# A graph-attention kernel: the first dense product as three rounded products, its operands transposed one tile ahead, the residual weights loaded later, TensorE's prologue reordered

## The chip, the cores and the metric

The kernel runs on one core of one Trainium2 chip. The metric is the device time of one execution in microseconds (us), the median of several executions.

## The reference

A graph has 1250 nodes of 768 features and 40,000 edges `(src, dst)`, to which one self loop per node is added. Two blocks follow each other, each `x = layernorm(x + block(x))`.

```python
x_norm = layer_norm(x, norm_g, norm_b)
out1 = gat_conv(x_norm, src, dst, W1, a_src1, a_dst1, b1, 4, 192, N)   # 4 heads
out2 = gat_conv(out1, src, dst, W2, a_src2, a_dst2, b2, 2, 96, N)      # 2 heads
block0 = concatenate([x, out2]) @ Wu + bu
# gat_conv: h = x @ W; e = leaky_relu(s_src[src] + s_dst[dst]);
#           softmax of e over the edges of one dst; sum of alpha * h[src]
h = relu(gcn_conv(x, W1, b1)); block1 = gcn_conv(h, W2, b2)   # second block
```

## The kernel before

The nodes are padded to T = 10 tiles of 128. The edges are turned into a dense matrix of counts, `ct`, of 1280 x 1280, which every later stage reads. All engines run one program each, written out in order, and meet at semaphores; what follows names the stages in order of time.

**Prologue.** SP loads W1 in two halves, small vectors, W2 (`w2x`), x (`xs`) and the upper 768 rows of Wu (`wux`). TensorE (`block.tensor`) transposes W1 into `w1T` (ScalarE copies each piece out of PSUM), transposes the edge keys (`keys()`, after VectorE has made `diag`), and forms twelve pieces of `wp` = W1 times W2 (n = 0 to 11, four PSUM banks in turn), which ScalarE copies to SBUF. VectorE works out which edge units each group needs (`cand` to `rngi`) and the layer norm of tile 0 (`moments`, `scales`; ScalarE's square root is `deviations`).

**Counting loop.** `tile(q)` runs for q = 0 to 9 with GPT = 4 groups w each. In a group VectorE writes one-hot matrices of edges (`one_hots`: `hots_*` and `hotd_*` for two windows of three edge units, then `xohs`, `xohd` for units that did not fit, in a loop whose length is read from `rngrow`). TensorE multiplies them into counts (`edge_group`), ScalarE copies the counts out (`ctmp`). Four windows of one-hots can be ready ahead of TensorE. Between the groups TensorE does the dense product of the tile, normalised x (transposed as `xT`) times `wp`, a quarter after each group: three products of 128x128 by 128x388 in float32, whose result `dense_out` copies to `g`. In the last tile the product is done in two halves after groups 0 and 1. At the head of a tile TensorE transposes the normalised rows `xh` (`normal_transposes`), and ScalarE scales them into `xT` (`transposed`); after group 0 TensorE transposes the counts of the tile before (`count_transposes`), of which ScalarE makes `mask` (`counts_out`). In its last group VectorE waits for the last `dense_out` (`source_scores`, `svec`).

**Between the loop and the heads.** VectorE runs `maxima(h)` for heads 0 to 3: ten instructions each (L590) that read two SBUF tensors, `src_row` and `mask`, back to back; `maxima(h)` needs the broadcast rows of head h, which TensorE makes (`source_rows`) and ScalarE copies. In TensorE's order these rows alternate with the residual product x times Wu (`x_wu(q)`, q = 0 to 4 with `wux`): source_rows of head 0, `x_wu(0)`, source_rows of head 1, and so on. Before `x_wu(0)` TensorE waits for `wu_plus`: GpSimd adds the identity to the six diagonal blocks of `wux` (L505), one instruction each, once it has landed. The first head's third tile on VectorE (`n == EARLY`) waits for `x_wu(4)`, since `att` takes the place of `wux`.

**Heads and second block.** Six attention heads (VectorE, ScalarE and TensorE in turn), then the graph convolution, in which each float32 product is already three products of rounded operands (`split_product`): high x high, high x low, low x high, with float32r operands.

## Time and profile before

| | |
|---|---|
| median of 3 runs | 799.88 us (799.39 to 800.42) |
| the profiled execution's own time | 799.75 us |
| its span | 798.0 us |
| TensorE (PE) busy | 753.3 us, 94% |
| VectorE (DVE) busy | 564.5 us, 71% |
| ScalarE (ACT) busy | 321.8 us, 40% |
| GpSimd (POOL) busy | 27.2 us, 3% |

The busy times are of the whole span; the counting loop takes about a fifth of it, and what limits it has to be read there. A float32 matmul appears as two records, a float32r one as one. "PEclk" is the granted TensorE clock as a share of the full one. In rows of the timeline the bracket names the idle time ahead of the instruction and what ended it; records overlap, so the pace is read from start to start.

### The profile page before, as it was taken

How to read it: one execution, taken by the hardware profiler on the slowest of the kernel's cores; microseconds unless marked ns; L12 is line 12 of the kernel's file. 1: busy time of each engine (PE TensorE's matmuls, PEld its weight loads, DVE VectorE, ACT ScalarE, POOL GpSimd, SP SyncE). 2: the span in 40 equal slices, each digit the busy share in tenths (PEclk: the TensorE clock that was granted, in tenths of full speed). 3: DMA queues.
4: the chain of work that ended last, by engine and by line, in shares of the span. 5: the costliest groups of instructions: out<-in, count | busy, mean ns of one | idle time of the engine just before them, and what ended most of it. 6: DMA issues, size and time to landing. Idle time of an engine off the chain costs nothing. (4 is left out here: it accounts for less than half of the span.)

```text
span 798.0 us, 12011 instructions
## 1 busy us (share of the span) xinstructions
PE 753.3 (94%) x4363; PEld 655.2 (82%) x4363; DVE 564.5 (71%) x972; ACT 321.8 (40%) x638; POOL 27.2 (3%) x41
## 2 busy tenths in 40 slices
PE   4899999998999989999998998899999999999997
PEld 2877677766666989999855888799999999999996
DVE  3498988872999999999689999695644332403554
ACT  2647767673533334444154454562203331301000
POOL 7100000000000020000000020000000000000000
PEclk8999999998989999999999999899999999999999
DMA  9400000000000231010000510100000003000111
GB/s 310 166 2 2 2 2 1 2 2 1 1 0 1 70 131 67 2 67 1 0 1 1 187 30 1 41 1 1 1 1 1 1 1 120 0 1 1 65 75 56
DMA packets 10673, 28.17 MB, mean 35 GB/s; under 512 B 675, under 2 KB 4079, under 8 KB 10100
## 3 DMA queue, kind: packets, MB, share of 16 engines
q1 hardware_dynamic: 9924, 27.04, 9.6%
q8 instruction: 38, 0.62, 0.3%
q10 hardware_dynamic: 688, 0.32, 0.2%
q14 instruction: 23, 0.19, 0.1%
HBM read 23.48 MB, written 3.88 MB: 34 GB/s over the span
## 5 line engine op out<-in xcount | busy, mean ns | idle before, releaser
L1260 PE MATMUL ps<-g,att 128*128 128x193 f32 x800 | 133.3, 328 | 3.7 <-DVE att L720 2.3
L1260 PEld LDWEIGHTS ps<-g,att 128*128 128x128 f32 x800 | 130.3, 190 | 6.5 <-DVE att L720 2.9
L1092 ACT ACTIVATE att<-att,ssrc 128x1250 f32<-128x1250 f32 x60 | 80.2, 1338 | 99.0 <-DVE att L759 98.8
L759 DVE SCALAR_TENSOR_TENSOR att<-uB,s 128x1250 f32<-128x1250 f32 x60 | 90.5, 1513 | 0.0
L1260 PE MATMUL ps<-wp,xT 128*128 128x388 f32 x240 | 87.5, 502 | 2.6 <-ACT xT L975 2.6
L1260 PE MATMUL ps<-ctr,yhi 128*128 128x512 f32 x360 | 88.1, 353 | 0.1
L720 DVE SCALAR_TENSOR_TENSOR att<-att,ct 128x1250 f32<-128x1250 f32 x60 | 87.2, 1454 | 0.7 <-ACT att L1092 0.5
L861 DVE TENSOR_TENSOR ylo_a<-ps,yhi 128x512 fp32r<-128x512 f32 (+2 forms) x34 | 16.1, 528 | 77.4 <-ACT yhi L943 77.4
L1260 PE MATMUL ps<-ctr,ylo_a 128*128 128x512 f32 (+3 forms) x288 | 70.2, 352 | 0.1
L1260 PEld LDWEIGHTS ps<-ctr,yhi 128*128 128x128 f32 x360 | 64.1, 188 | 6.0 <-issue 0.4
L1260 PEld LDWEIGHTS ps<-wp,xT 128*128 128x128 f32 x240 | 42.6, 190 | 26.1 <-issue 3.7
L1260 PEld LDWEIGHTS ps<-ctr,ylo_a 128*128 128x128 f32 x288 | 51.0, 188 | 5.2 <-DVE ylo_a L854 0.4
L943 ACT ACTIVATE yhi<-ps 128x384 fp32r<-128x384 f32 (+2 forms) x36 | 16.3, 529 | 95.6 <-PE ps L1260 95.6
L1260 PE MATMUL ps<-h2x,att 128*128 128x97 f32 x400 | 48.1, 277 | 4.2 <-DVE att L720 2.8
L1260 PEld LDWEIGHTS ps<-h2x,att 128*128 128x128 f32 x400 | 46.0, 192 | 6.9 <-DVE att L720 5.9
L1260 PE MATMUL ps<-wux,xTd 128*128 128x384 f32 x120 | 40.8, 500 | 0.7 <-ACT xTd L943 0.7
L1260 PE MATMUL ps<-wux,xT 128*128 128x384 f32 x120 | 40.9, 497 | 0.0
L1260 PE MATMUL ps<-gw2lo,yhi 128*128 128x384 f32 x120 | 40.6, 338 | 0.0
L1260 PE MATMUL ps<-gw2hi,yhi 128*128 128x384 f32 x120 | 40.4, 337 | 0.0
L1260 PE MATMUL ps<-gw1lo,yhi 128*128 128x384 f32 x120 | 40.2, 335 | 0.0
L899 DVE SCALAR_TENSOR_TENSOR hpre<-ps,dinv,gb1b 128x384 f32<-128x384 f32 x20 | 12.4, 618 | 37.8 <-PE ps L1260 37.8
L1260 PEld LDWEIGHTS ps<-wux,xTd 128*128 128x128 f32 x120 | 23.3, 197 | 16.6 <-issue 2.3
(244 smaller groups left out, 1332.3 us busy)
## 6 DMA issues: line engine op xcount, KB each, us to landing
uB<-u_dram SPq DMA_DIRECT2D x4, 1280.0 KB, 5.9
wux<-in_L_gnn_Wu SPq DMA_DIRECT2D x2, 2304.0 KB, 15.2
gw<-in_L_gnn_W SPq DMA_DIRECT2D x2, 2304.0 KB, 10.7
xs<-in_x SPq DMA_DIRECT2D x1, 3456.0 KB
out<-ybuf SPq DMA_DIRECT2D x9, 384.0 KB, 2.3
w<-in_L_gnn_W SPq DMA_DIRECT2D x2, 1152.0 KB, 7.8
w2x<-in_L_gnn_W SPq DMA_DIRECT2D x1, 576.0 KB, 9.8
wuo<-in_L_gnn_Wu SPq DMA_DIRECT2D x1, 576.0 KB
```

The costliest lines, as they stand in the source:

```text
L720: v.scalar_tensor_tensor(a, a, HUGE, ct[:, q, 0:N], ALU.min, ALU.mult).then_inc(att_ready, 1)
L759: v.scalar_tensor_tensor(att[:, att_place(n), 0:N], uB[:, hp % 2, 1, 0:N], s08[:, h, q:q + 1], uB[:, hp % 2, 0, 0:N], ALU.add, ALU.max).th ...
L861: last = v.tensor_tensor(rows, place(f, k)[:, a0 * P - span[0]:a1 * P - span[0]].rearrange("p (t n) -> p t n", n=P), yhi[:, a0:a1, f * P:( ...
L899: v.scalar_tensor_tensor(hpre[:, n % 2, :], ps[:, H_RING[n % 4], 0:HALF], dinv[:, q:q + 1], gb1b[:, k * HALF:(k + 1) * HALF], ALU.mult, AL ...
L943: a.activation(dst, src, ACT.Copy, **kw).then_inc(done, 1)
L1092: a.activation(at_, at_, ACT.Exp, bias=ssrc[:, h, q:q + 1]).then_inc(att_exp, 1)
L1260: return t.matmul(o, lhsT, rhs, start=start, stop=stop, **kw)
```

## The change

The dense product of the counting loop is done as three products of rounded operands. ScalarE's copy of a piece of the weights now rounds to `wphi`, and VectorE subtracts it from PSUM to get `wplo` (`weights_low`, twelve pieces, in the prologue; a bank is free for the next piece only then). For x, ScalarE makes `xThi` by one more copy, and VectorE makes `xTlo` (`x_low`, once per tile, after group 0). The normalised rows are transposed and scaled during the tile before (after group 1 on TensorE, ahead of group 2's outputs on ScalarE). The moments of tiles 1 and 2 move from the loop into the prologue. On TensorE the transposes of the edge keys stand behind both halves of W1, and the two products with `diag` behind the small vectors. `wplo` takes the room of `wux`, so the load of `wux` waits until the last dense product is done. Line numbers of the changed kernel are about 35 higher (the helper L1260 is L1296, L590 is L625 or so).

```diff
+            xin = t_in["x"]
+            sp.dma_start(xs[:, 0, :], xin[0:P, :]).then_inc(x0_in, 16)
             sp.dma_start(w2x[:, :, 0:C1], t_in["L0_gnn_W2"].rearrange("(j p) n -> p j n", p=HC)).then_inc(w2_in, 16)
-            xin = t_in["x"]
-            sp.dma_start(xs[:, 0:T - 1, :], xin[0:(T - 1) * P, :].rearrange("(t p) n -> p t n", p=P)).then_inc(x_in, 16)
+            sp.dma_start(xs[:, 1:T - 1, :], xin[P:(T - 1) * P, :].rearrange("(t p) n -> p t n", p=P)).then_inc(x_in, 16)
             sp.wait_ge(pad_set, 2)
             sp.dma_start(xs[0:NR, T - 1, :], xin[(T - 1) * P:N, :]).then_inc(x_in, 16)
-            sp.dma_start(wux[:, :, :], t_in["L0_gnn_Wu"][0:D, :].rearrange("(k p) n -> p k n", p=P)).then_inc(wux_in, 16)
             sp.wait_ge(rng_ready, 1)
             sp.dma_start(rngrow[0:1, :], rngi[:, :]).then_inc(rng_row_in, 16)
+            sp.wait_ge(dn_ps, 2 * T)
+            sp.dma_start(wux[:, :, :], t_in["L0_gnn_Wu"][0:D, :].rearrange("(k p) n -> p k n", p=P)).then_inc(wux_in, 16)
...
+            def weights_low(n0, n1):
+                for n in range(n0, n1):
+                    k, hh = n // 2, n % 2
+                    v.wait_ge(wp_out, n + 1)
+                    v.tensor_tensor(wplo[:, k, 2 * hh:2 * hh + 2, :], ps[:, n % 4, 0:2 * GW].rearrange("p (h n) -> p h n", h=2),
+                                    wphi[:, k, 2 * hh:2 * hh + 2, :].bitcast(F32), ALU.subtract).then_inc(wplo_out, 1)
+            def x_low(q):
+                x32, low, high = (xT0[:, :, :], xT0lo[:, :, :], xT0hi[:, :, :]) if q == 0 else (xT[:, q % 2, :, :], xTlo[:, q % 2, :, :], xThi[:, q % 2, :, :])
+                v.wait_ge(xhi_out, q + 1)
+                v.tensor_tensor(low, x32, high.bitcast(F32), ALU.subtract).then_inc(xlo_out, 1)
...
+            v.wait_ge(const_b, 1)
+            v.wait_ge(x0_in, 16)
+            moments(0, 1)
             v.wait_ge(keys_t, 1)
             v.tensor_copy(sloT[:, :, :].rearrange("p a c -> p (a c)"), ps[:, 5, 0:EC]).then_inc(keys_out, 1)
+            v.wait_ge(keys_t, 2)
...
+            weights_low(0, 1)
...
+            weights_low(1, 2)
...
+            scales(0, 1)
+            weights_low(2, 6)
             v.wait_ge(x_in, 32)
-            moments(0, 1)
-            scales(0, 1)
+            moments(*pair(0))
+            weights_low(6, 8)
+            scales(*pair(0))
+            v.memset(svec[:, :].bitcast(F32), 0.0)
+            v.memset(uvecs[:, :].bitcast(F32), 0.0)
+            v.tensor_tensor(sel[:, :], identf[0:VR, 0:H1 * T], identf[0:VR, VLO:VR], ALU.add)
+            weights_low(8, 2 * KD)
...
-                    if win == RING - 1:
-                        v.wait_ge(wp_out, 2 * KD)
...
-                    if q < T // 2 and w == 0:
+                    if w == 0:
+                        x_low(q)
+                    if 0 < q < T // 2 and w == 0:
                         moments(*pair(q))
-                    if q < T // 2 and w == 2:
+                    if 0 < q < T // 2 and w == 2:
...
+                a.wait_ge(tp_out, 2 * q + 2)
+                copy(high, dst, xhi_out)
+            deviations(0, 1)
             for k in range(KD):
                 for hh in range(2):
                     n = 2 * k + hh
                     a.wait_ge(wp_ps, n + 1)
-                    copy(wp[:, k, 2 * hh:2 * hh + 2, :], ps[:, n % 4, 0:2 * GW].rearrange("p (h n) -> p h n", h=2), wp_out)
-                    if n == 7:
-                        deviations(0, 1)
-                    if n == 8:
-                        a.wait_ge(x_in, 32)
+                    copy(wphi[:, k, 2 * hh:2 * hh + 2, :], ps[:, n % 4, 0:2 * GW].rearrange("p (h n) -> p h n", h=2), wp_out)
+                    if n == 5:
+                        a.wait_ge(x0_in, 16)
                         a.wait_ge(rstd_ready, 1)
                         a.activation(xh0[:, :], xs[:, 0, :], ACT.Identity, bias=nmr[:, 0:1], scale=rstd[:, 0:1]).then_inc(xh_ready, 1)
-                    if n == 10:
-                        transposed(0, xT0)
-            a.wait_ge(wp_out, 2 * KD)
+                    if n == 8:
+                        a.wait_ge(rng_ready, 1)
+                        transposed(0, xT0[:, :, :], xT0hi[:, :, :])
+                    if n == 9:
+                        deviations(1, 3)
...
+            a.wait_ge(wplo_out, 2 * KD)
...
-                if q > 0:
-                    transposed(q, xT[:, r, :, :])
                 for w in range(GPT):
-                    if q < T // 2 and w == 1:
+                    if 0 < q < T // 2 and w == 1:
                         deviations(2 * q + 1, min(2 * q + 3, T))
-                    if w == GPT - 1 and not last:
+                    if w == 0 and not last:
                         a.wait_ge(rstd_ready, q // 2 + 2)
-                        fixed_place(q + 1, 1 - r)
+                        fixed_place(q + 1)
+                    if w == 2 and not last:
+                        transposed(q + 1, xT[:, 1 - r, :, :], xThi[:, 1 - r, :, :])
...
+            t.wait_ge(const_a, 1)
+            t.wait_ge(keys_made, 1)
+            for gi in range(EG):
+                t.transpose(ps[:, 4, gi * P:(gi + 1) * P], shir[:, gi, :], identf[:, :])
+                last = t.transpose(ps[:, 5, gi * P:(gi + 1) * P], slor[:, gi, :], identf[:, :])
+            last.then_inc(keys_t, 1)
...
+            t.wait_ge(diag_ready, 1)
+            for k in range(2):
+                last = mm(ps[0:NG, 6 + k, 0:EG * P], ones[:, 0:NG], diag[:, k, :], True, True)
+            last.then_inc(keys_t, 1)
...
-                if k == 2:
-                    t.wait_ge(keys_out, 1)
                 for hh in range(2):
                     n = 2 * k + hh
                     if n >= 4:
-                        t.wait_ge(wp_out, n - 3)
+                        t.wait_ge(wplo_out, n - 3)
...
-                    if n == 9:
-                        t.wait_ge(rng_ready, 1)
+                    if n == 7:
+                        t.wait_ge(keys_out, 1)
                         normal_transposes(0, xh0)
...
-                if q > 0:
-                    t.wait_ge(cp_deg, 3 * q + 1)
-                    normal_transposes(q, xh[:, r, :])
+                high, low = (xT0hi[:, :, :], xT0lo[:, :, :]) if q == 0 else (xThi[:, r, :, :], xTlo[:, r, :, :])
                 if q == 1:
                     t.wait_ge(cst_out, 1)
                 for w in range(GPT):
...
                         cs = range(KD) if last else range(3 * (w % 2), 3 * (w % 2) + 3)
                         if 0 in cs:
                             t.wait_ge(dn_out, 2 * q + k + 1)
-                        t.wait_ge(tp_out, 2 * q + (1 if cs[-1] < 3 else 2))
+                        t.wait_ge(xlo_out, q + 1)
                         for c in cs:
-                            step = mm(ps[:, 2 + k, 0:2 * GW], xT0[:, c, :] if q == 0 else xT[:, r, c, :], wp[:, c, 2 * k:2 * k + 2, :], c == 0, c == KD - 1, skip_group_check=True)
+                            mm(ps[:, 2 + k, 0:2 * GW], high[:, c, :], wphi[:, c, 2 * k:2 * k + 2, :], c == 0, False, skip_group_check=True)
+                            mm(ps[:, 2 + k, 0:2 * GW], high[:, c, :], wplo[:, c, 2 * k:2 * k + 2, :], False, False, skip_group_check=True)
+                            step = mm(ps[:, 2 + k, 0:2 * GW], low[:, c, :], wphi[:, c, 2 * k:2 * k + 2, :], False, c == KD - 1, skip_group_check=True)
                         if cs[-1] == KD - 1:
                             step.then_inc(dn_ps, 1)
                     if w == 0 and behind:
                         t.wait_ge(tp_out, 2 * q + 2)
                         count_transposes(q - 1, 1 - r)
+                    if w == 1 and not last:
+                        t.wait_ge(cp_deg, 3 * q + 4)
+                        normal_transposes(q + 1, xh[:, :])
```

TensorE's queue, one group of the first tile and what follows it, before (rows of `order` carry the name of the output and the inputs):

```order
L1260 MATMUL ps<-identb 128x2x16
L1260 MATMUL ps<-wp,xT_65 128x388 x3
L1260 MATMUL ps<-hotd_b,hots_b 128x160 x6
L321 TENSOR_LOAD rngrow
L1260 MATMUL ps<-hotd_c,hots_c 128x160 x6
```

And the same place now:

```order
L1296 MATMUL ps<-identb 128x2x16
L1296 MATMUL ps<-wphi,xT0hi 128x388 [waits xlo_out,dn_out]
L1296 MATMUL ps<-wplo,xT0hi 128x388
L1296 MATMUL ps<-wphi,xT0lo 128x388
L1296 MATMUL ps<-wphi,xT0hi 128x388
```

Three products have become nine, of three operand pairs in turn, and the first waits for VectorE's `x_low`.

SP's queue from the load of W2 on, before:

```order
L426 DMA w2x<-in_L_gnn_W 96x8x192
L428 DMA xs<-in_x 128x9x768
L430 DMA xs<-in_x 98x768 [waits pad_set]
L431 DMA wux<-in_L_gnn_Wu 128x6x768
L433 DMA rngrow<-rngi 1x40x2 [waits rng_ready]
```

And now:

```order
L434 DMA xs<-in_x 128x768
L435 DMA w2x<-in_L_gnn_W 96x8x192
L436 DMA xs<-in_x 128x8x768
L438 DMA xs<-in_x 98x768 [waits pad_set]
L440 DMA rngrow<-rngi 1x40x2 [waits rng_ready]
L442 DMA wux<-in_L_gnn_Wu 128x6x768 [waits dn_ps]
```

The first tile of x comes ahead of W2, and `wux` has moved behind a wait that ends with the last dense product. VectorE's queue in a tile of the loop now, between the last one-hot of group 0 and the first of group 1:

```order
L630 TENSOR_TENSOR xohd<-vkey,key 128x320
L654 ISA
L654 COMPARE_AND_BRANCH
L542 TENSOR_TENSOR xTlo<-xT,xThi 128x768 [waits xhi_out]
L548 BN_STATS stats<-xs 128x6 x4
```

The row of L542 is new; before, the moments (tiles 1 to 4) or the next one-hot followed at once.

## Rows read from the trace of the kernel before

**Rows 1.** Timeline of TensorE in a late tile: start, length, engine, line, instruction.

```profile
120.32 2.19 PE L1260 MATMUL ps<-wp,xT 128*128 128x388 f32 x6 [0.17 <-ACT xT L975]
122.35 1.25 PE L1368 MATMUL ps<-identf,ctmp 128*128 128x128 f32 x10
...
134.65 2.19 PE L1260 MATMUL ps<-wp,xT 128*128 128x388 f32 x6 [0.17 <-ACT xT L975]
```

**Rows 2.** Busy time in stretches: PE, PEld, DVE, ACT, POOL, clock, DMA.

```profile
90.00:105.30 15.30, 14.90 (x100) 10.54 (x100) 13.64 (x35) 10.49 (x29) 0.00 (x0) 1.00 0.01 2
```

**Rows 3.** VectorE's waits, 39.28 to 180: total us, times, longest.

```profile
DVE xohs L594 <- issue: 7.7, 32, 0.6
...
DVE hots_b L594 <- PE ps L1260: 3.2, 5, 1.2
DVE hots_a L594 <- PE ps L1260: 1.8, 5, 0.6
DVE rstd L571 <- ACT sd L968: 1.5, 2, 0.9
DVE xohs L594 <- PE ps L1260: 0.8, 2, 0.6
```

**Rows 4.** Timeline of VectorE at both ends of the loop.

```profile
39.28 0.56 DVE L594 TENSOR_TENSOR hots_a<-iota,sloT 128x768 bf16<-128x768 bf16 x1 [0.55 <-DVE key L632]
...
179.76 0.33 DVE L595 TENSOR_TENSOR xohd<-vkey,key  x1
```

**Rows 5.** Timeline of TensorE in the second block's split product.

```profile
609.72 0.34 PE L1260 MATMUL ps<-gw1hi_b,yhi 128*128 128x384 f32 x1
...
614.96 0.33 PE L1260 MATMUL ps<-gw1hi_a,yhi 128*128 128x384 f32 x1
```

**Rows 6.** Instructions by tile `gw`: ns min/median/max, first and last start.

```profile
L806 DVE TENSOR_TENSOR gw1lo<-gw,gw1hi_a x4: 948/952/953, 566.0 to 568.6; 128x768 fp32r<-128x768 f32 x4
```

**Rows 7.** Timeline of TensorE in the last tile.

```profile
184.78 4.16 PE L1260 MATMUL ps<-wp,xT 128*128 128x388 f32 x12
...
195.21 0.20 PE L1260 MATMUL ps<-identb 128*128 128x32 bf16 x1
```

**Rows 8.** Timeline of the prologue.

```profile
16.33 0.45 PE L1276 MATMUL ps<-identf,shir 128*128 128x128 f32 x1 [5.16 <-DVE diag L532]
...
20.44 2.83 PE L1292 MATMUL ps<-identf,w 128*96 128x128 f32 x24
...
24.94 13.40 PE L1260 MATMUL ps<-w2x,w1T 96*128 96x194 f32 x80 [0.45 <-ACT acol L943]
...
42.41 1.94 DVE L560 BATCH_NORM_STATS2 stats<-xs 128x6 f32<-128x384 f32 x4
```

**Rows 9.** Timeline between the loop and the first head.

```profile
198.22 1.46 DVE L590 CUSTOM_DVE_ANT_0 scrap<-ssB_a,mask 128x1250 bf16<-128x1250 f32 x1 [3.87 <-ACT ssB_a L943]
...
201.81 7.98 PE L1260 MATMUL ps<-wux,xTd 128*128 128x384 f32 x24 [0.67 <-ACT xTd L943]
...
213.65 1.46 DVE L590 CUSTOM_DVE_ANT_0 scrap<-ssB_a,mask 128x1250 bf16<-128x1250 f32 x1
...
245.72 8.87 PE L1260 MATMUL ps<-wux,xTd 128*128 128x384 f32 x27
...
255.12 0.16 DVE L758 MEMSET att<- 128x120 f32 x1
```

**Rows 10.** Timeline of GpSimd's second set of adds and VectorE meanwhile.

```profile
290.18 4.40 POOL L505 TENSOR_TENSOR wux<-wux,identf 128x128 f32<-128x128 f32 x6 [257.88 <-DMA wux<-in_L_gnn_Wu]
...
290.75 1.46 DVE L720 SCALAR_TENSOR_TENSOR att<-att,ct 128x1250 f32<-128x1250 f32 x1
```

**Rows 11.** Instructions by tile `wux`: ns min/median/max, first and last start.

```profile
L505 POOL TENSOR_TENSOR wux<-wux,identf x12: 449/453/2337, 29.8 to 294.1; 128x128 f32<-128x128 f32 x12
```

**Rows 12.** DMA issues, 655 to 680: size, us to landing.

```profile
gw<-in_L_gnn_W SPq DMA_DIRECT2D x1, 2304.0 KB, 8.3
```

**Rows 13.** Busy time behind the loop's end; columns as in Rows 2.

```profile
195.00:200.00 5.00, 4.99 (x25) 4.80 (x24) 1.78 (x3) 1.91 (x4) 0.00 (x0) 0.50 0.00 0
```

More of the change, by code:

```diff
@@ L519, in _, with moments @@
             S, Dn = edges[:, :, 0, :], edges[:, :, 1, :]
+            def weights_low(n0, n1):
[8 more added lines that the diff above has]
+                v.tensor_tensor(low, x32, high.bitcast(F32), ALU.subtract).then_inc(xlo_out, 1)
+            def moments(q0, q1):
+                for q in range(q0, q1):
+                    for k in range(2):
+                        last = v.bn_stats(stats[:, q, k, :], xs[:, q, k * HALF:(k + 1) * HALF])
+                last.then_inc(stats_own, 1)
+                v.wait_ge(stats_own, (q0 + 1) // 2 + 1)
+                for q in range(q0, q1):
+                    last = v.bn_aggr(mv[:, q, :], stats[:, q, :, :])
+                last.then_inc(var_ready, 1)
             v.wait_ge(const_a, 1)
@@ L1297, in _ @@
             t.transpose(ps[0:HC, 1, 0:3 * NJ], arows[:, :], identf[0:3 * NJ, 0:3 * NJ]).then_inc(vec_t, 1)
+            t.wait_ge(diag_ready, 1)
+            for k in range(2):
+                last = mm(ps[0:NG, 6 + k, 0:EG * P], ones[:, 0:NG], diag[:, k, :], True, True)
+            last.then_inc(keys_t, 1)
             t.wait_ge(vec_out, 1)
```

65 lines of the change are left out of this document (24 added, 41 removed).

## The prediction, before the run

> **What bounds the kernel now.** The busy shares say TensorE (94%), but they are a mean over stages, so I read the counting loop by itself first. The timeline of TensorE shows a late tile [rows 1]: the next one begins 134.65 - 120.32 = 14.33 us on, almost without a gap, so there TensorE sets the pace. An early tile takes 15.30 us, of which VectorE is busy 13.64 [rows 2]; the rest of it is mostly VectorE's own gaps, 7.7 / 32 = 0.24 us ahead of each `xohs` with no engine to wait for [rows 3]. So tiles 1 to 4 run at VectorE's pace already, and over the whole loop it waits for others only 3.2 + 1.8 + 1.5 + 0.8 = 7.3 us [rows 3]. From its first one-hot at 39.28 to the end of the last tile's third group at 179.76 + 0.33 = 180.1 it needs 140.8 us [rows 4]. TensorE is some way behind and ends the last dense product at 184.78 + 4.16 = 188.9; the loop ends at 195.4, 6.5 us later [rows 7]. After it VectorE runs `maxima` back to back, and TensorE alternates rows and `x_wu` [rows 9]. At the third tile of the first head both arrive together: `x_wu(4)` ends at 245.72 + 8.87 = 254.6, VectorE is there at 255.12 [rows 9]. TensorE's slack between loop and heads is 0.5 us.
>
> **The dense products.** Three float32 products take about 2.04 us (122.35 - 120.32) [rows 1], 0.68 each. The second block does the same three-product form with 384 columns: 30 records from 609.72 to 614.96, 0.175 each [rows 5]. Nine are 1.57 us, so a quarter is 0.46 us shorter, and 40 quarters (ten tiles of four) 18.6 us. ScalarE's `xT` for the first quarter, 0.17 us late per tile now [rows 1], is ready a tile ahead. This is all TensorE's time, and it counts only as far as VectorE can follow.
>
> **What VectorE gets.** `x_low` is one subtraction of 128x768 from SBUF per tile. The same form on `gw` starts three more times in 568.6 - 566.0 us, 0.87 each [rows 6]; I take 0.9, ten times, +9.0 us. In six tiles (0 and 5 to 9) it fills a gap of 0.24 that stood there: -1.4. The moments of tiles 1 and 2 leave the loop: 1.94 [rows 8] and about 0.5 for the small operations behind them, -2.4. Waits for TensorE and ScalarE vanish, 7.3 us over 14 times, but the twelve on TensorE fall back to the usual gap: -(7.3 - 12 x 0.24) = -4.4. Sum for the stretch of 140.8: 141.6 us. In a tile VectorE then needs 14 to 16 us and TensorE about 12.2 (14.33 less 4 x 0.46 and 0.17), so VectorE sets the pace throughout.
>
> **The prologue.** TensorE was idle 5.16 us before the keys [rows 8]. Now the second half of W1 (2.83 us) fills that, ending at 14.0; keys and `diag` took 20.44 - 16.33 = 4.1 us [rows 8], so the pieces of W1 x W2 begin at 18 to 19 instead of 24.94. Each takes 13.40 / 10 = 1.34 us [rows 8]. The ninth ends, with the six transposes put ahead of it, at about 31; behind its copy ScalarE scales `xT0`, rounds it, copies another piece and takes the square root (about 4.5 us, one after another); VectorE waits for that, then has the small operations and four subtractions of 0.45: about 38.0, and with key and register loads the first one-hot at 38.8, 0.5 earlier. Six us on TensorE become half a us on VectorE. Bounds: 37.8 and 40.5 (if the clock falls in between).
>
> **The loop's end.** The third group of the last tile is ready at 38.8 + 141.6 = 180.4, the second 3.1 us (a quarter of VectorE's tile without extras) before. Around it TensorE has a first half (18 products, 3.15 us), the transposes of counts (1.25 [rows 1]), a group (1.0) and the second half (3.15); from the first group of the tile, 174.5, that makes 183.0 against 188.9. The rest, 6.5 us, stays. So the loop ends 6 us earlier (bounds 3 and 8.5).
>
> **Where it is given back.** `wux` used to be there since the prologue. Now SP issues it when the last dense product is done, 183.1. A load of the same size with the queues free lands 8.3 us after its issue [rows 12]: 191.4. VectorE begins `maxima(0)` 198.22 - 188.94 = 9.3 us after the dense product [rows 9], at 192.3. GpSimd has six adds, 2.5 us where nothing disturbs them (median 453 ns, shortest 449) [rows 11], so only two are done when `maxima(0)` begins. What then? One add took 2337 ns, and it is the first of the second set [rows 11]: it began at 290.18, and 2.34 - 0.45 = 1.9 us later, 292.1, is the time at which the VectorE instruction of 290.75 ended, 292.2 [rows 10]. That instruction read two SBUF tensors, as the one before it did. GpSimd had been waiting since before 290.75 and still did not get in between the two. `maxima(0)` is ten such instructions end to end, 13.9 us. I therefore take the four adds left as held up until 206.2 and done at 207.9.
>
> The Trainium skill ("SBUF — State Buffer", Who interferes with whom) says that a VectorE instruction with two SBUF inputs and a GpSimd one that reads SBUF exclude each other for one instruction at a time. By that alone GpSimd would get its turn after each of the ten, which is the third case below and gives about 798; the row shows a turn that it did not get.
>
> TensorE would have begun `x_wu(0)` at 201.81 - 6 = 195.8; it begins at 207.9, 6.1 us later than before. It was idle for 12 us, and behind a lesser lull the granted clock was 0.50 for 5 us [rows 13], so up to 1.8 us more. The rows of head 1 stand behind `x_wu(0)` in TensorE's queue: they are out 7.5 + 2.3 us after 207.9, at 217.7 to 219.5, against VectorE's old start of `maxima(1)` at 213.65 [rows 9], +4 to +6. TensorE reaches the end of `x_wu(4)` 6.1 to 7.9 us later, less the slack of 0.5. I take +6.2 for the first head; from there all is as before. 799.75 + 6.2 = 806 us. The profiled execution (799.75, span 798.0) is within 0.2 us of the median of 799.88, so the sum serves for both.
>
> **Rivals.**
> (1) GpSimd is not held up, or keeps its turn once it has it, since its adds begin 0.8 us before `maxima(0)`. Then `wux` is complete 8.4 + 2.5 = 10.9 us after the dense product, and TensorE asks for it only at 201.81 - 188.94 = 12.9: the 6 us stay. At worst VectorE waits 1.8 us for the last four adds. 793.8 to 795.6; I write 794.5. For it: nothing shows this very instruction (L590) against GpSimd. This is the case on the other side; it decides at whether the sixth add is done within 12.9 us. Chance 0.30.
> (2) GpSimd gets one add in after each instruction of `maxima(0)`: four times 1.38 + 0.42 = 7.2, complete at 16.6 after the dense product, 3.7 late for TensorE, up to 1.8 for the clock: -6 + 3.7 to 5.5, 797.5 to 799.3. Chance 0.12.
> (3) TensorE still sets the loop, or VectorE's gaps shrink with the waits: at most 18.6 + 2 us less, 779, or the same less 13 if the adds are held up. Against it stands [rows 2]. Chance 0.03.
> (4) The loop gains nothing: with the half clock of [rows 13] in the early tiles, where TensorE would be idle about 3 us behind each `x_low` and the moments, and no hold-up later. 799 to 803. Against it: four windows ready ahead let TensorE make it up. Chance 0.07.
> (5) The forecast, 804 to 808. Chance 0.48.
>
> **How the numbers follow.** The likeliest is (5), 806, with a range of its own of 803 to 809 (loop bounds 3 and 8.5, clock 0 or 1.8). The 80% range must reach rival (1): 793 to 808.5. A measurement of this kernel tells about 0.2% (1.6 us) from no change. Faster: (1), (3), half of (2): 0.40. Same: half of (2), part of (4): 0.09. Slower: (5) and the rest of (4): 0.51.
>
> **What the profile after would show.** Right: nine records of `wphi`/`wplo` per quarter in 1.57 us; VectorE over 93% busy in the loop with gaps only of its own, PE waiting for DVE in each tile; the loop's end near 189.5; `wux` landing 8 to 9 us after the dense product; GpSimd's third add several us long, up to the end of `maxima(0)`; TensorE idle 10 us or more ahead of `x_wu(0)`, and VectorE idle ahead of `maxima(1)`. Wrong: adds of 0.45 us during `maxima(0)` (then rival 1 or 2), a tile below 14 us (rival 3), or the first one-hot after 41.

## The result, and the profile after

The changed kernel takes 795.67 us (median of 4 runs, 793.24 to 796.2) against 800.15 us for the kernel before on the same chip: a ratio of 0.993, 95% interval 0.991 to 0.995. A second set of runs, beside other kernels, gave 0.993 again (0.992 to 0.995). It is faster by 0.7%, where I had forecast 806 us and slower. The profiled execution took 793.24 us (span 791.3) against 799.75.

VectorE at both ends of the loop, to be held against [rows 4] (timeline: start, length, engine, line, instruction, idle time ahead):

```profile
37.49 0.56 DVE L629 TENSOR_TENSOR hots_a<-iota,sloT 128x768 bf16<-128x768 bf16 x1 [0.26 <-DVE key L665]
...
173.99 0.32 DVE L630 TENSOR_TENSOR xohd<-vkey,key  x1
```

The first one-hot comes 1.8 us earlier, the third group of the last tile ends at 174.3 instead of 180.1. The stretch between takes 136.8 us instead of 140.8; I had forecast 141.6.

TensorE at the end of the last dense product and behind the loop, against [rows 7] and [rows 9]:

```profile
178.07 0.34 PE L1296 MATMUL ps<-wphi,xTlo 128*128 128x388 f32 x1
178.25 0.96 PE L1296 MATMUL ps<-hotd_a,hots_a 128*128 128x160 bf16 x11
...
188.75 1.49 PE L1453 MATMUL ps<-identf,xs 128*128 128x128 f32 x6
194.32 9.82 PE L1296 MATMUL ps<-wux,xTd 128*128 128x384 f32 x24 [4.08 <-POOL wux L514]
```

The same place in the kernel before, behind its last dense product:

```profile
188.78 1.02 PE L1260 MATMUL ps<-hotd_a,hots_a 128*128 128x160 bf16 x12
```

The dense products end at 178.25, where the next product starts, against 188.78 (the 188.94 of [rows 7] is the end of the last record, which overlaps that start). The gain is 10.5 us, not 6. But `x_wu(0)` begins at 194.32 after 4.08 us of waiting for GpSimd, only 7.5 earlier, and takes 9.82 us instead of 7.98. The cause stands on VectorE's and GpSimd's timelines (against [rows 9] and [rows 10]):

```profile
187.32 1.74 DVE L625 CUSTOM_DVE_ANT_0 scrap<-ssB_a,mask 128x1250 bf16<-128x1250 f32 x1 [3.91 <-ACT ssB_a L975]
...
188.99 1.70 DVE L625 CUSTOM_DVE_ANT_0 scrap1b<-ssB_a,mask 128x1250 bf16<-128x1250 f32 x1
...
190.62 1.70 DVE L625 CUSTOM_DVE_ANT_0 scrap<-ssB_a,mask 128x1250 bf16<-128x1250 f32 x1
...
195.52 1.45 DVE L625 CUSTOM_DVE_ANT_0 scrap1b<-ssB_a,mask 128x1250 bf16<-128x1250 f32 x1
196.90 0.08 DVE L625 DVE_READ_ACCUMULATOR2_ANT mx<- 128x1 f32 x1
196.90 1.45 DVE L625 CUSTOM_DVE_ANT_0 scrap<-ssB_a,mask 128x1250 bf16<-128x1250 f32 x1
...
205.97 1.46 DVE L625 CUSTOM_DVE_ANT_0 scrap<-ssB_a,mask 128x1250 bf16<-128x1250 f32 x1 [1.95 <-ACT ssB_a L975]
...
248.72 0.16 DVE L790 MEMSET att<- 128x120 f32 x1 [1.25 <-PE ps L1296]
```

```profile
186.88 7.39 POOL L514 TENSOR_TENSOR wux<-wux,identf 128x128 f32<-128x128 f32 x6 [169.90 <-DMA wux<-in_L_gnn_Wu]
```

The six adds last 7.39 us instead of the 2.51 of the first set before the change. While they last, the instructions of `maxima(0)` start every 1.63 us (188.99 to 190.62), and every 1.38 afterwards (195.52 to 196.90). So VectorE and GpSimd take turns: one add at each handover, which costs VectorE 0.25 us. (Two of the six adds fall ahead of it and at its start, the other four at the next four handovers.) VectorE then waits 1.95 us for the rows of head 1, which stand behind `x_wu(0)`, and 1.25 us for `x_wu(4)`. The heads begin 6.4 us earlier than before (248.72 against 255.12). Of the 10.9 us that `maxima(0)` had won (187.32 against 198.22), about 4.5 are given back: 1.3 for the adds (five pitches of 1.63 to 1.67 instead of 1.38), 1.95 and 1.25 for the two waits.

The load of `wux` (issue and landing, against [rows 12]), and the waits of VectorE from 37.5 to 174.4 (total us, times, longest), against [rows 3]:

```profile
wux<-in_L_gnn_Wu SPq DMA_DIRECT2D x1, 2304.0 KB, 8.4
```

```profile
DVE xohs L629 <- issue: 6.3, 26, 0.6
DVE hots_a L629 <- issue: 2.9, 11, 0.6
DVE hots_a L629 <- PE ps L1296: 0.7, 3, 0.2
```

VectorE waits for TensorE only 0.7 us in the loop now, and its own gaps are smaller too (6.3 us ahead of `xohs` against 7.7), although ten `x_low` have come in. The dense products themselves look as forecast (timeline of TensorE in a late tile, against [rows 1] and [rows 5]):

```profile
130.36 0.42 PE L1296 MATMUL ps<-wphi,xThi 128*128 128x388 f32 x1
130.62 0.33 PE L1296 MATMUL ps<-wplo,xThi 128*128 128x388 f32 x1
...
131.85 0.34 PE L1296 MATMUL ps<-wphi,xTlo 128*128 128x388 f32 x1
132.03 1.25 PE L1400 MATMUL ps<-identf,ctmp 128*128 128x128 f32 x10
```

Nine products take 132.03 - 130.36 = 1.67 us, the first of them 0.26, the others 0.176. The three float32 ones took 2.03 [rows 1].

### The profile page after: what moved, and what is told of

Same layout as the page of the kernel before. It is cut to its first block and busy times, and to the rows that moved or that the text cites. A ratio compares the mean times of both kernels' runs of the same rounds, so it can differ in the third digit from the quotient of the medians.

```text
span 791.3 us, 12286 instructions
## 1 busy us (share of the span) xinstructions
PE 745.6 (94%) x4483; PEld 675.2 (85%) x4483; DVE 578.4 (73%) x994; ACT 328.9 (42%) x648; POOL 32.2 (4%) x41
## 5 line engine op out<-in xcount | busy, mean ns | idle before, releaser
L1296 PE MATMUL ps<-g,att 128*128 128x193 f32 x800 | 133.5, 328 | 3.2 <-DVE att L752 1.8
L1296 PEld LDWEIGHTS ps<-g,att 128*128 128x128 f32 x800 | 130.4, 190 | 6.0 <-DVE att L752 3.3
L1296 PE MATMUL ps<-ctr,yhi 128*128 128x512 f32 x360 | 88.1, 353 | 0.0
L1296 PE MATMUL ps<-ctr,ylo_a 128*128 128x512 f32 (+3 forms) x288 | 70.2, 352 | 0.1
L1296 PEld LDWEIGHTS ps<-ctr,yhi 128*128 128x128 f32 x360 | 64.1, 188 | 5.9 <-issue 0.3
L1296 PEld LDWEIGHTS ps<-ctr,ylo_a 128*128 128x128 f32 x288 | 51.0, 188 | 5.2 <-DVE ylo_a L886 0.4
L1296 PE MATMUL ps<-h2x,att 128*128 128x97 f32 x400 | 48.1, 277 | 4.2 <-DVE att L752 2.8
L1296 PEld LDWEIGHTS ps<-h2x,att 128*128 128x128 f32 x400 | 46.0, 192 | 6.9 <-DVE att L752 5.9
L1296 PE MATMUL ps<-wux,xTd 128*128 128x384 f32 x120 | 42.0, 511 | 4.1 <-POOL wux L514 4.1
L1296 PEld LDWEIGHTS ps<-wux,xTd 128*128 128x128 f32 x120 | 23.9, 203 | 20.5 <-POOL wux L514 4.5
L1296 PE MATMUL ps<-wux,xT 128*128 128x384 f32 x120 | 41.4, 502 | 0.0
L1296 PE MATMUL ps<-gw2lo,yhi 128*128 128x384 f32 x120 | 40.6, 338 | 0.0
L1296 PE MATMUL ps<-gw2hi,yhi 128*128 128x384 f32 x120 | 40.4, 337 | 0.0
L1296 PE MATMUL ps<-gw1lo,yhi 128*128 128x384 f32 x120 | 40.2, 335 | 0.0
L1296 PE MATMUL ps<-wphi,xThi 128*128 128x388 f32 x108 | 39.8, 368 | 0.0
L1296 PE MATMUL ps<-wplo,xThi 128*128 128x388 f32 x108 | 37.2, 344 | 0.0
## 6 DMA issues: line engine op xcount, KB each, us to landing
gw<-in_L_gnn_W SPq DMA_DIRECT2D x2, 2304.0 KB, 10.6
```

The costliest lines, as they stand in the source:

```text
L1296: return t.matmul(o, lhsT, rhs, start=start, stop=stop, **kw)
```

## Experiments

Each starts from the changed kernel. Behind the loop, theory A says that the turns between the adds and `maxima(0)` cost what is given back, its rival B that the late landing or the half clock does. In the loop, theory C says that TensorE paces the late tiles, D that VectorE paces them all, and S, formed later, that VectorE's own gaps run beneath its work. E to H are about when GpSimd gets its turn.

**1. Without the adds, and with the adds on VectorE.**

```diff
                 pool.wait_ge(loaded, 16)
+                if wu is wux:
+                    pool.sem_inc(wu_plus, KD)
+                    continue
```

> The changed kernel without GpSimd's six adds to wux (the residual x is left out of x times Wu for the first five tiles); TensorE is released when wux has landed. Theory A (the adds, in turns with maxima(0), cost what is given back after the loop): landing near 187, TensorE asks for wux at 190.2 and doesn't wait, maxima(0) keeps a pitch of 1.38, the heads begin 57.2 us after maxima(0) as before the change, at 244.5 instead of 248.5, and the time is 3 to 4 us below the changed kernel's 793 to 796, so 789.5 to 792. Theory B (the late landing, or the half clock behind the lull, costs it): TensorE still waits or x_wu(0) still takes 9.8 us, the heads begin after 247, and the time is at most 1.5 us lower.

Measured: 789.48 us, ratio 0.985 (0.983 to 0.987). The heads begin at 245.28, 3.4 us earlier than in the changed kernel.

```diff
-            for wu, loaded in ((wux, wux_in), (wux2, wux2_in)):
+            for wu, loaded in ((wux2, wux2_in),):
...
+            v.wait_ge(wux_in, 16)
+            for k in range(KD):
+                block_k = wux[:, k, k * P:(k + 1) * P]
+                v.tensor_tensor(block_k, block_k, identf[:, :], ALU.add).then_inc(wu_plus, 1)
             maxima(0)
```

> The six adds are done by VectorE, after wux has landed and ahead of maxima(0). Theory A: they take 0.2 us each, 1.2 in all, from 187 on; maxima(0) begins near 188.5 with a pitch of 1.38, TensorE doesn't wait, the heads begin near 245.7, time 2.5 to 3 us below the changed kernel, 790.5 to 793. Theory B: the same start of the heads as in the changed kernel, 248.5, within 1 us, and no gain.

Measured: 790.25 us (789.93 to 790.41), ratio 0.987 (0.985 to 0.989). The heads begin at 245.48. VectorE's timeline of this kernel, and TensorE's behind it:

```profile
187.37 1.30 DVE L732 TENSOR_TENSOR wux<-wux,identf 128x128 f32<-128x128 f32 x6 [4.07 <-DMA wux<-in_L_gnn_Wu]
188.59 1.45 DVE L625 CUSTOM_DVE_ANT_0 scrap<-ssB_a,mask 128x1250 bf16<-128x1250 f32 x1
189.97 0.08 DVE L625 DVE_READ_ACCUMULATOR2_ANT mx<- 128x1 f32 x1
189.97 1.45 DVE L625 CUSTOM_DVE_ANT_0 scrap1b<-ssB_a,mask 128x1250 bf16<-128x1250 f32 x1
```

```profile
190.75 9.84 PE L1300 MATMUL ps<-wux,xTd 128*128 128x384 f32 x24 [0.67 <-ACT xTd L979]
```

The six adds take 1.22 us on VectorE, the pitch is 1.38 from the first instruction on, and TensorE doesn't wait for them. Theory A holds for 3.2 to 3.4 us of the 4.5. Theory B is right in one part: `x_wu(0)` still takes 9.8 us (granted clock 0.50 from 190 to 194), so the half clock there isn't a result of waiting for the adds. VectorE's wait for `x_wu(4)` is 1.05 us without the adds, so of the 1.25 us above only 0.20 went with them; with the adds on VectorE, which starts `maxima(0)` 1.3 us later, there is no such wait.

**2. One float32 product, and two products instead of three.**

```diff
-                            mm(ps[:, 2 + k, 0:2 * GW], high[:, c, :], wphi[:, c, 2 * k:2 * k + 2, :], c == 0, False, skip_group_check=True)
...
+                            step = mm(ps[:, 2 + k, 0:2 * GW], high[:, c, :].bitcast(F32), wphi[:, c, 2 * k:2 * k + 2, :].bitcast(F32), c == 0, c == KD - 1, skip_group_check=True)
```

> The changed kernel with each dense product as one float32 product of the rounded operands (the low parts are computed but not multiplied), all else as changed. Theory C (TensorE sets the pace of tiles 5 to 9 after the change too, at 13.08 us a tile, VectorE that of tiles 0 to 4): late tiles take 14.2 to 14.4 us, early ones stay at 15.8 to 16.1; the last dense product ends at 184 to 186 instead of 178.25 (before the change 188.9). Theory D (VectorE paces all tiles of the changed kernel, and TensorE's shorter products gained little): late tiles near 13.3, last dense product before 181.

Measured: 802.38 us, ratio 1.0025 (1.001 to 1.004), so slower than before the change. The last dense product ends at 185.58, and TensorE's late tiles take 14.27 us (134.69 to 148.96 between two sets of count transposes). The loop of this profile and of the next began 0.46 us later than that of the changed kernel (the key of tile 0 at 37.40 against 36.94), and that has to come off every end compared here: 6.9 us are the products'.

```diff
-                            mm(ps[:, 2 + k, 0:2 * GW], high[:, c, :], wplo[:, c, 2 * k:2 * k + 2, :], False, False, skip_group_check=True)
```

> The changed kernel without the product of the high x with the low weights (left out of the result): TensorE has 60 x 4 products fewer, VectorE the same work. Theory C: tiles 5 to 8 go from 13.08 to VectorE's own pace of 12.6 to 12.9, so with the last half's own 1.07 us the last dense product ends at 175.5 to 176.5. Theory D: nothing but the last half's own 1.07: 177.2. A loop that TensorE paced throughout would end 6 x 4 x 0.178 = 4.3 us earlier in the late tiles alone: before 173.

(The numbers of products in this expectation are off: it is 12 fewer in a tile, 2.1 us.) Measured: 792.28 us, ratio 0.989 (0.987 to 0.991); the last dense product ends at 175.78, 2.9 us earlier once the start is taken off. That is the time that theory C gave, but not by its way: the table below shows that VectorE's tiles did not move, so it is TensorE's lag behind VectorE that shrank.

**3. Half of `x_low`, and more work for VectorE.**

```diff
-                v.tensor_tensor(low, x32, high.bitcast(F32), ALU.subtract).then_inc(xlo_out, 1)
+                v.tensor_tensor(low[:, 0:3, :], x32[:, 0:3, :], high[:, 0:3, :].bitcast(F32), ALU.subtract).then_inc(xlo_out, 1)
```

> VectorE subtracts only half of x_low (128x384 instead of 128x768), and TensorE multiplies that half twice (the low part of x is wrong by that). VectorE has 0.45 us less in each of ten tiles, TensorE the same work. Theory C (VectorE paces tiles 0 to 4, TensorE tiles 5 to 8 at 13.08 us): tiles 0 to 4 become 0.4 to 0.5 shorter, 15.4 to 15.6, tiles 5 to 8 stay at 13.0 to 13.1; the last dense product ends 2.0 to 2.4 us earlier, at 175.9 to 176.3. Theory D (VectorE paces every tile): 4 us earlier, 174.2. A loop that TensorE paced throughout would not move.

TensorE multiplies the one half twice (`low[:, c % 3, :]`). Measured: 795.0 us, ratio 0.993 (0.991 to 0.995); the last dense product ends at 176.59.

```diff
                     if w == 0:
                         x_low(q)
+                    if q >= T // 2 and w == 0:
+                        again = xThi[:, q % 2, :, :].bitcast(F32)
+                        v.tensor_tensor(mask[:, T - 1, 0:D].rearrange("p (k c) -> p k c", k=KD), again, again, ALU.subtract)
```

> A second subtraction of 128x768 (a scratch result that nothing reads) behind x_low in tiles 5 to 9 only; all results as changed. Theory S (in the late tiles VectorE is paced neither by TensorE nor by the sum of its instructions, but by what stands between them, loop ends and register loads, which runs on beneath the data instructions): a good part hides, VectorE's gaps in tiles 5 to 8 shrink, and the tiles grow from 13.0 by 0.2 to 0.6 us. Theory D (sum of its own instructions and fixed gaps): the tiles grow by the whole 0.9, to 13.9, the third group of the last tile comes 4.5 us later. Theory C (TensorE sets 13.08 with room to spare on VectorE): they don't grow at all.

The second of the two runs differs in `w == 2`:

> The same extra subtraction in tiles 5 to 9, behind group 2 instead of group 0. Theory S: it hides as far as a gap follows it, tiles 13.2 to 13.7. Theory D: 13.9. Theory C: 13.1.

Measured, one run each: 799.51 and 798.5 us, both with a late `wux` (10.7 and 9.2 us to land), so the times are not compared. The loop is read from the starts of VectorE's `key` instruction, one per tile, in the timelines (us; the last column is the start of what follows the product):

| kernel | tile 0 | tiles 1 to 4 | tiles 5 to 8 | last dense product ends |
|---|---|---|---|---|
| before | 12.51 | 60.80 | 54.33 | 188.78 |
| changed | 9.47 | 63.22 | 51.56 | 178.25 |
| one float32 product | 9.46 | 64.10 | 53.34 | 185.58 |
| two products | 9.47 | 63.21 | 51.56 | 175.78 |
| half `x_low` | 9.46 | 61.64 | 51.55 | 176.59 |
| 0.95 us more behind group 0, tiles 5 to 9 | 9.46 | 63.51 | 51.80 | not compared |
| 0.96 us more behind group 2, tiles 5 to 9 | 9.46 | 63.19 | 52.56 | not compared |

Tiles 1 to 4 answer to VectorE's work alone: the halved `x_low` (559 ns instead of 959) takes 1.58 us off four tiles, its whole 0.40 each, and fewer products take nothing off. (Tile 1 alone differs by up to 0.3 us between kernels that are the same up to there.) Tiles 5 to 8 answer to neither: 51.56 with a sixth less on TensorE (2.1 us of 13.1 in a tile), 51.55 with 0.40 less on VectorE, and 51.80 with 3.8 us more on VectorE in the four. The last is the clearest, though the extra work does not vanish everywhere. Tile by tile the changed kernel takes 12.59, 12.93, 13.06 and 12.98; with the work behind group 0 it is 13.01, 13.11, 12.94 and 12.74, and with the work behind group 2 13.46, 12.95, 13.11 and 13.04. The first tile that has it pays 0.4 or 0.9 us, the next three together -0.2 and +0.1. VectorE's idle time in the four tiles fell from 4.1 to 2.2 us (work behind group 0); the rest of the 3.8 us shows as starts that stand closer together, `xohd` to `key` 0.24 us instead of 0.31 for instance. VectorE's gaps (waits of VectorE from 110 to 165) were, in the changed kernel and then with the extra work behind group 0:

```profile
DVE xohs L629 <- issue: 2.9, 11, 0.6
DVE hots_a L629 <- issue: 1.2, 5, 0.3
```

```profile
DVE xohs L629 <- issue: 0.8, 4, 0.2
DVE xohs L629 <- PE ps L1299: 0.6, 1, 0.6
DVE hots_a L629 <- issue: 0.5, 2, 0.3
```

So theory D falls in these tiles, and theory C by the two products, which left every tile of VectorE's the same within 0.01 us. By the size of the growth alone (0.06 and 0.25 us a tile) the last two runs stand nearer to theory C's nothing than to the 0.2 to 0.6 and 0.2 to 0.7 that I had put for S. What is shown of theory S is that VectorE's gaps are not time that is added to its instructions. Something paces tiles 6 to 8 at 12.7 to 13.1 us, and data instructions fit into it as long as they leave a gap. That this is VectorE's own loops and register loads is the likely reading, since nothing in the profile is waited for there, but it was not tried by itself. TensorE's own 13.08 us stand close to it, and extra work together with two products, which would part the two, was not run. With the float32 product TensorE's 14.27 us become the pace again at the end of the stretch (VectorE's tiles 7 and 8 take 13.59 and 14.22).

**4. TensorE's order behind the loop, and in the prologue.**

```diff
             x_transposes(0)
+            t.wait_ge(cp_deg, 3 * T + 4)
+            source_rows(3, 6)
             t.wait_ge(wu_plus, KD)
             x_wu(0)
-            t.wait_ge(cp_deg, 3 * T + 4)
...
-                source_rows(3 * q, 3 * q + 3)
+                if q > 1:
+                    source_rows(3 * q, 3 * q + 3)
```

> On TensorE the broadcast rows of head 1 stand ahead of x_wu(0) instead of behind it; the adds stay on GpSimd. Theory A (TensorE idles 4.1 us for the adds, and the rows behind it make VectorE wait 1.95 us for maxima(1)): 2.2 of the 4.1 us are filled with the rows, VectorE's 1.95 vanish, the pitch in the first maxima stays 1.63, x_wu(4) ends about 2 us earlier; the heads begin near 246.7 instead of 248.7, time 1.5 to 2 us below the changed kernel. Rival: the rows' copies on ScalarE and the half clock eat it, and the heads begin after 248.

Measured: 793.87 us, ratio 0.9915 (0.990 to 0.993), not to be told from the changed kernel. In its profile TensorE waited 3.7 us for ScalarE's count copies ahead of the rows, which I had overlooked, and 2.4 us for GpSimd; `wux` had landed late there (10.7 us) and the heads began at 251.87. The rival's number is met, but the late landing alone would meet it: the changed kernel with the same late landing (10.6 us, part 5) began its heads at 254.60, 2.7 us later, and its `maxima(1)` at 211.45 instead of 204.53. So the new order gains in the heads what theory A says, when like is held against like; the medians (793.87 against 795.14 in part 5) do not tell it from nothing.

```diff
             for j in range(NJ):
+                if j == NJ // 2:
+                    t.wait_ge(const_a, 1)
+                    t.wait_ge(keys_made, 1)
...
+                    last.then_inc(keys_t, 1)
...
-            t.wait_ge(const_a, 1)
-            t.wait_ge(keys_made, 1)
...
```

> The changed kernel with TensorE's old prologue order: transposes of the edge keys and the products with diag between the two halves of W1. If that order is worth what TensorE gained there (the pieces of W1 x W2 from 24.94 to 17.6), the pieces begin 3 to 7 us later, and since VectorE waits for all twelve (weights_low) the first one-hot comes 2.5 to 5 us later than 37.49, at 40 to 42.5, and the last dense product by as much. Rival (the prologue is bound on VectorE and ScalarE, and the reorder brought only a fraction of its 7 us, as I put it before the run): the first one-hot at 38 to 39.5.

Measured: 802.96 us, ratio 1.004 (1.0025 to 1.006). The first one-hot comes at 45.02, 7.5 us later, more than I had put. The pieces of W1 x W2 begin at 24.04 instead of 17.63, and VectorE waits 6.80 us for ScalarE's first `wphi`. Part of that is TensorE's clock: with the old order TensorE is idle for 2.18 us ahead of the keys, and the granted clock from 15 to 20 is 0.50, as before the change; in the changed kernel it is 1.00 there. The products with `diag`, here and then in the changed kernel:

```profile
16.23 2.78 PE L1296 MATMUL ps<-diag,ones 128*40 128x384 f32 x4 [1.30 <-DVE diag L567]
```

```profile
16.22 1.48 PE L1296 MATMUL ps<-diag,ones 128*40 128x384 f32 x4 [0.95 <-DVE diag L567]
```

The order of the prologue is worth as much here as the shorter products.

**5. The changed kernel again.**

> The changed kernel once more, beside the others on one chip. 0.992 to 0.995 of the time before; in the profile the same starts in the loop within 0.2 us, and the heads from 248.5 to 250.

Measured: 795.14 us (794.58 to 799.82, 7 runs), ratio 0.993 (0.992 to 0.995). The profiled execution was the longest of them, 799.82, and it shows where the spread comes from. The loop is the same within 0.03 us up to the key of the last tile (161.19), but `wux` needed 10.6 us to land:

```profile
wux<-in_L_gnn_Wu SPq DMA_DIRECT2D x1, 2304.0 KB, 10.6
```

```profile
189.17 9.46 POOL L514 TENSOR_TENSOR wux<-wux,identf 128x128 f32<-128x128 f32 x6 [172.18 <-DMA wux<-in_L_gnn_Wu]
```

```profile
211.45 1.46 DVE L625 CUSTOM_DVE_ANT_0 scrap<-ssB_a,mask 128x1250 bf16<-128x1250 f32 x1 [7.21 <-ACT ssB_a L975]
```

Landing 2.3 us later, all six adds fell under `maxima(0)`, TensorE waited 8.44 us instead of 4.08, VectorE 7.21 instead of 1.95, and the heads began at 254.60 instead of 248.72: a landing 2.3 us late cost 5.9, of the 6.6 us by which this execution was longer than the first profiled one (793.24).

**6. Why GpSimd got its turns.**

```diff
+                if h == 0:
+                    v.scalar_tensor_tensor(place[:, 0:N], src_row(h)[:, 0:N], -FAR, mask[:, q, 0:N], ALU.max, ALU.subtract).then_inc(mx_done, 1)
+                    return
...
+            v.memset(mx[:, 0, :], 0.0)
             maxima(0)
```

> The ten instructions of maxima(0) are replaced by ten scalar_tensor_tensor ones on the same two SBUF tensors, without the read-out of an accumulator behind each (the maxima of head 0 are left out and set to zero); the six adds stay on GpSimd. Theory E (in my row of before GpSimd was passed over since one VectorE instruction followed the other with nothing between them; in maxima(0) it gets its turn at the read-out of the accumulator): now the adds that are not done when the chain begins are held up to its end, near 201: TensorE waits 10 us or more for GpSimd instead of 4.1 to 8.4, the pitch of the chain stays at its undisturbed 1.4. Rival F (turns are taken between any two instructions, or the row of before was a start too late for that handover alone): one add per instruction as before, pitch 0.25 longer while the adds last, TensorE's wait 4 to 8.5 us.

Measured, one run: 797.42 us. The adds take 9.23 us, the pitch is 1.63 while they last and 1.37 behind them, and TensorE waits 7.3 us. Theory E falls.

The same with `accum_out=zz[:, q:q + 1]`:

> As the run without an accumulator, but the ten scalar_tensor_tensor write an accumulator (to a scratch column; the maxima of head 0 are again zero), so that its read-out stands behind each. Theory E: turns are taken as in maxima(0), pitch 0.25 longer while the adds last, TensorE waits 4 to 8.5 us. Another theory (it is the kind of instruction, not the read-out, that lets GpSimd in): the same as without the accumulator.

Measured, one run: 795.42 us, adds 8.62 us, TensorE waits 5.4: the same turns.

Then the two forms of [rows 10] themselves, both writing float32:

```diff
+                if h == 0:
+                    if q % 2 == 0:
+                        v.scalar_tensor_tensor(wide_scrap[:, q % 2, 0:N], src_row(h)[:, 0:N], epsc[:, 0:1], src_row(h)[:, 0:N], ALU.add, ALU.max).then_inc(mx_done, 1)
+                    else:
+                        v.scalar_tensor_tensor(wide_scrap[:, q % 2, 0:N], src_row(h)[:, 0:N], HUGE, mask[:, q, 0:N].bitcast(U16), ALU.min, ALU.mult).then_inc(mx_done, 1)
+                    return
```

> The ten instructions of maxima(0) are replaced by the two forms between which GpSimd was passed over in the trace of before, in the same order: the first of a head (two float32 inputs and a scalar per partition, float32 output), then the second (float32 and 16-bit inputs, float32 output), to a scratch (the maxima of head 0 are left out and set to zero). Six adds stay on GpSimd. Theory G (the forms decide: there is no turn between a first and a second form): a turn only every other instruction, 2.8 us apart, so six adds take up to 14 to 17 us and TensorE waits 9 to 13. Rival H (something else in that place decided, and any handover is a turn): 7.4 to 9.5 us for the adds, TensorE waits 4 to 8.5.

Measured, one run: 799.73 us, and on VectorE's timeline:

```profile
188.80 1.46 DVE L630 SCALAR_TENSOR_TENSOR wide_scrap<-ssB_a,mask 128x1250 f32<-128x1250 f32 x1
190.18 1.71 DVE L628 SCALAR_TENSOR_TENSOR wide_scrap<-ssB_a,epsc 128x1250 f32<-128x1250 f32 x1
191.81 1.71 DVE L630 SCALAR_TENSOR_TENSOR wide_scrap<-ssB_a,mask 128x1250 f32<-128x1250 f32 x1
193.44 1.71 DVE L628 SCALAR_TENSOR_TENSOR wide_scrap<-ssB_a,epsc 128x1250 f32<-128x1250 f32 x1
```

Each handover is a turn, in both directions. The adds take 9.75 us and TensorE waits 8.5, at or just above rival H's upper bounds (`wux` landed after 10.4 us) and below theory G's 9. Ten of the first form alone:

> As the alternating run, with ten of the first form. Theory G in the version that a first form gives up no turn at its end: the adds are held up to the end of the chain, 201 to 202, and TensorE waits 11 us or more. In the version that a second form takes none at its start, and rival H: 7.4 to 9.5 us for the adds, TensorE waits 4 to 8.5.

Ten of the second:

> As the alternating run, with ten of the second form. Theory G in the version that a second form lets nothing in ahead of it: held up to the end of the chain, TensorE waits 11 us or more. In the other version, and rival H: 7.4 to 9.5 us for the adds, TensorE waits 4 to 8.5.

Measured, one run each: 795.35 and 797.53 us, the adds take 8.60 and 9.93 us, TensorE waits 5.5 and 8.7. Theory G falls in every version, and rival H stands, its upper bounds a little low.

**7. A version that beats both.** The adds on VectorE as in 1, behind the first instruction of `maxima(0)`:

```diff
-            maxima(0)
+            maxima(0, 0, 1)
+            v.wait_ge(wux_in, 16)
...
+            maxima(0, 1, T)
```

> A version meant to be faster: the six adds on VectorE, behind the first instruction of maxima(0) instead of ahead of it, so that a landing up to 1.4 us later than maxima(0)'s start costs nothing, and TensorE, which asks for wux at 190.2 to 190.8, has it at 190.0. Heads at 245.3 to 245.7 as with the adds ahead (245.48), time the same as there within 0.5 us, ratio 0.986 to 0.988, with a narrow spread; 3 to 5 us below the changed kernel.

Measured: 790.83 us (789.66 to 793.55), ratio 0.986 (0.9845 to 0.988), the same as with the adds ahead. In its profile `wux` landed after 10.4 us, and the heads still began at 245.78: the landing that cost the changed kernel 5.9 us costs 0.3 here. The spread is not as narrow as I had put it: this execution, of 793.55 us, was 3.6 us longer than the profiled one with the adds ahead, though its heads began only 0.3 later, so the rest of that arose behind this point. TensorE's `x_wu(0)` ran here at the full clock:

```profile
190.90 7.98 PE L1301 MATMUL ps<-wux,xTd 128*128 128x384 f32 x24 [0.67 <-ACT xTd L980]
```

It took 1.86 us less than in experiment 1 with the adds ahead, and the heads began no earlier for it. Once the adds are on VectorE, the half clock in this stretch costs nothing, which settles the other part of theory B.

## Why the prediction was wrong

**Right.** Nine products in 1.57 us (measured 1.67); TensorE able to start on W1 x W2 at 18 to 19 (17.63), which becomes far less on VectorE (-0.5 forecast, -1.8 measured); `x_low` at 0.9 us (0.96, or 0.87 from start to start); `wux` landing 8 to 9 us after its issue (8.4, in part luck: in eight of the 17 traces of changed kernels it took more than 9); 1.8 us for the half clock in `x_wu(0)` (9.82 against 7.98); the adds colliding with `maxima(0)`, TensorE waiting for them, and VectorE then waiting for `maxima(1)`. The keys and `diag` I had priced at 4.1 us from a row in which the granted clock was 0.50; with TensorE kept busy it was 1.00, and `diag` took 1.48 us instead of 2.73.

**The step that turned the sign: "I therefore take the four adds left as held up until 206.2".** They were done at 194.27. GpSimd gets one add in at every handover, as the runs of part 6 show with five kinds of chain. I had read one row, an add passed over at a handover of [rows 10], as a rule. It recurs in the second set of adds of each of the 18 traces, begun 0.53 to 0.74 us ahead of the same instruction; yet an add begun 0.69 us ahead got its turn in experiment 6, and the same two forms of instructions let adds in. Why it is passed over at that one place stays open. One difference was not tried: there the instruction writes over its own input `att`, which ScalarE has just written, while those of experiment 6 read `ssB_a` and write a scratch. The Trainium skill ("SBUF — State Buffer", Who interferes with whom) says that the two engines exclude each other for an instruction at a time, and by that alone the case was my rival 2. These traces agree with it: pitch 1.63 instead of 1.38, one add per instruction. Without the false step the sum would have been my own -6 with rival 2's delay, 797.5 to 799.3.

**The term that was mis-sized: "Sum for the stretch of 140.8: 141.6 us".** It was 136.8. VectorE's busy time rose by 4.7 us (120.57 to 125.24 in that stretch), not by 6.6, and its idle time fell by 8.7 (from 20.25 to 11.57), not by 5.8. I had treated the gaps ahead of `xohs` as a fixed toll on each tile and let `x_low` fill one of 0.24 us. Part 3 shows that they are not: in tiles 6 to 8 a whole further instruction of 0.95 us disappears in them. So a shorter `x_low` was worth its full 0.40 us only in tiles 1 to 4, beside the moments, and nothing in the late tiles, where VectorE had also been held by TensorE before. I had also taken "14 to 16 us" a tile for VectorE throughout, from the mean of the stretch; its tiles 5 and 6 already took 12.9 us each before the change (124.69 - 111.75 and 137.57 - 124.69). "A tile below 14 us" was my own sign for rival 3, "VectorE's gaps shrink with the waits", at a chance of 0.03. It came true: that mechanism, though not the size that I gave it, is what the loop shows. "VectorE sets the pace throughout" was right for the early tiles. For the late ones I had TensorE at 12.2 us a tile (by its own terms 12.3); it needs 13.08, with no idle time to speak of (busy 51.04 of 51.56 us). A quarter became only 0.37 us shorter rather than 0.46, which is 0.4 of the missing 0.9; the rest I have not taken apart.

**The loop's end: -6 forecast, -10.5 measured.** It adds up from the starts in the table: key of tile 0 -1.5 (36.94 against 38.44), tile 0 -3.0, tiles 1 to 4 +2.4, tiles 5 to 8 -2.8, the last tile up to its third group -0.9 (13.1 against 14.0), and TensorE's lag behind that -4.7 (3.9 against 8.7). In tile 0 the moments and their small operations took 2.5 us with them (2.4 forecast), `x_low` brought 0.9, and 1.4 went out of the gaps. The lag is the largest part of the gain, but not of my error: I had it fall by 6.2, to 2.6 (183.0 against 180.4). The error is VectorE's third group, 0.3 us later by my sum and 5.8 earlier in fact (174.3): 1.3 of it from the start of the loop and 4.8 from the stretch, less 1.5 on the lag. A TensorE that had fallen behind in the late tiles hardly does now, and does its last two halves in 0.7 us less each.

**Rival 1** (794.5, 0.30) came nearest in time, but not in its mechanism: the adds did not stay out of the way, the loop had won more. That my range holds the measured time is luck: its lower end was rival 1's, which assumed away the collision that the profile shows, while the forecast's own two errors, the hold-up too dear and the loop too slow, added up to 10 us. The measured case is rival 2's mechanism with a loop end 4.5 us better than forecast. The balance: the shorter products are worth 6.9 us at the end of the last dense product (185.58 less the 0.46 of its later start, against 178.25), the prologue's order 7.5 us at the first one-hot, and without either the change is slower than before (experiments 2 and 4). Behind the loop 4.5 us are given back in the profiled execution, of which experiment 1 puts 3.2 to 3.4 on the adds (5 to 6 in the medians, whose landings of `wux` are not known).

## What to carry to other kernels

Before an added instruction is charged to an engine, look at whether its gaps shrink when work is put beside them: an idle gap with nothing to wait for may take up further work, and only adding or halving work in that very stretch tells. Hold executions against each other only where the same transfer took the same time, or the late landing passes for the effect. One row in which an engine loses a turn is not a rule for a chain; price the case of turns as well, and see how far the work ahead of it depends on when a transfer lands. When a late transfer feeds work of GpSimd that meets two-input work of VectorE, try those few instructions on VectorE itself: here 1.2 us there replaced 7.4 to 9.5 on GpSimd.

## What the runs showed of the hardware

- A GpSimd add of 128x128 (0.45 us alone) against VectorE instructions with two SBUF inputs of 1250 columns: one add per instruction, VectorE 0.25 us longer for each, six adds in 7.39 to 9.93 us. It is the same for the maximum with its accumulator's read-out and for plain two-input instructions without one. The exception is the first add of the second set, 2.29 to 2.51 us long in all 18 traces.
- The load of `wux`, 2304 KB, issued behind the last dense product in all the changed kernels, landed after 8.3 to 10.7 us from run to run.
- `x_wu(0)` took 9.8 us after TensorE had waited 4.1 us, also 9.8 without that wait, and 10.99 behind a wait of 7.3 us; in the run of part 7 it took 7.98, with a granted clock of 1.00 from 190 to 200 where the others had 0.50 in a part of it. What decides that was not tried.
- In the prologue the granted clock from 15 to 20 was 0.50 where TensorE had idled 5.16 us (before) or 2.18 us (old order, part 4) ahead of the keys, and 1.00 in the changed kernel, whose TensorE had worked without a gap from 9.74 to 14.6.
